# One-core graph network on edge ends: projections written out without loops, aggregations with a narrow end-row product and byte masks

## The reference, cut to what matters

```python
x = x + L0(relu(layernorm(x)))   # 3 rounds: h = h + sigmoid(GAT(h)), one head
x = x + L1(relu(layernorm(x)))   # relational conv, 4 bases
x = x + L2(relu(layernorm(x)))   # GAT, 8 heads, linear
x = x + L3(relu(layernorm(x)))   # edge messages and mean
# GAT(x): h = x @ W; s = h @ a_src; d = h @ a_dst
#   e = leaky(s[src] + d[dst]), softmax over the edges of each dst and a self loop
#   out[n] = sum(alpha * h[src]) + alpha_self * h[n] + b
```

## Time and profile before

| | us |
|---|---|
| median of three runs | 4129.71 (4114.74 to 4135.91) |
| the profiled execution | 4123.5 |
| its span, first to last instruction | 4121.8 |
| TensorE, VectorE, ScalarE, GpSimd busy | 2421.4, 2277.9, 1509.5, 2159.3 |

### The profile page before, as it was taken

The page is one execution under the profiler, slowest core; times in us unless marked ns, Lnnn a source line. Parts: engine busy times, 40 slices in busy tenths (PEclk is TensorE's granted clock), DMA queues, the critical chain, the costliest instruction groups (busy, mean ns, idle before and its releaser), DMA issues. The chain is left out here.

```text
span 4121.8 us, 57885 instructions
## 1 busy us (share of the span) xinstructions
PE 2421.4 (59%) x13649; PEld 1953.8 (47%) x13649; DVE 2277.9 (55%) x7669; ACT 1509.5 (37%) x3239; POOL 2159.3 (52%) x1921
## 2 busy tenths in 40 slices
PE   1136899999996647466465637775636444433433
PEld 1123676667676546466454634454626332322222
DVE  3145999899896655223423448885674333333223
ACT  0006999999994641121122013222420022222100
POOL 3628675557645850350064236555820278877755
PEclk9998999999998875686588559887865576666655
DMA  2140132333212537441654363323312533333243
GB/s 61 31 167 24 47 103 88 90 96 106 88 51 67 143 100 228 140 123 47 177 152 109 112 187 95 95 86 87 111 29 81 151 74 72 73 70 72 53 137 114
DMA packets 570788, 405.84 MB, mean 98 GB/s; under 512 B 51549, under 2 KB 497702, under 8 KB 570146
## 3 DMA queue, kind: packets, MB, share of 16 engines
q1 hardware_dynamic: 513650, 356.21, 28.7%
q0 software_dynamic: 56000, 46.29, 6.0%
q10 hardware_dynamic: 880, 0.41, 0.0%
HBM read 270.38 MB, written 158.24 MB: 104 GB/s over the span
## 5 line engine op out<-in xcount | busy, mean ns | idle before, releaser
L1147 POOL DMA_INDIRECT p_ends_state<-t_d,p_ends_ix x300 | 316.0, 1053 | 568.0 <-issue 279.7
L806 POOL TENSOR_TENSOR a_rs<-a_ve,w_neg_half 128x16 f32<-128x16 f32 x113 | 330.4, 2924 | 243.1 <-DVE a_ve L742 211.8
L1367 PE MATMUL p_pm<-w_aug,p_ht 128*128 128x130 f32 (+1 forms) x1600 | 327.9, 326 | 165.1 <-ACT p_ht L1321 107.4
L832 ACT ACTIVATE a_nr<-a_xb,a_nm,a_rs 128x128 f32<-128x128 f32 x882 | 370.4, 488 | 26.1 <-POOL a_nm L808 26.1
L1972 POOL DMA_INDIRECT e_a<-t_d,e_ix x200 | 209.4, 1047 | 298.1 <-DMA e_a<-t_s 235.9
L1367 PEld LDWEIGHTS p_pm<-w_aug,p_ht 128*128 128x128 f32 x1600 | 272.0, 231 | 187.0 <-issue 135.1
L894 PE MATMUL a_ps<-w_ident,a_nr 128*128 128x128 f32 x1568 | 247.7, 282 | 126.7 <-ACT a_ht L840 47.0
L902 PE MATMUL a_ps<-a_ht,w_aug 128*128 128x512 f32 x588 | 316.8, 624 | 2.4 <-DVE a_ht L709 2.4
L894 PEld LDWEIGHTS a_ps<-w_ident,a_nr 128*128 128x128 f32 x1568 | 181.9, 144 | 275.8 <-issue 243.1
L1697 PE MATMUL c_ps<-layer_src,c_sel 128*128 (+1 forms) x800 | 192.0, 419 | 192.3 <-DMA c_sel<-t_sel 107.8
L709 DVE TENSOR_TENSOR a_ht<-a_ps,a_ht 128x512 f32<-128x512 f32 x294 | 201.9, 688 | 135.2 <-ACT a_ps L847 117.8
(11 more groups left out here) (362 smaller groups left out, 6724.9 us busy)
## 6 DMA issues: line engine op xcount, KB each, us to landing
t_s<-p_ends_state SPq DMA_DIRECT2D x100, 256.0 KB
c_sel<-t_sel SPq DMA_DIRECT2D x100, 256.0 KB
c_a<-t_d SPq DMA_DIRECT2D x100, 256.0 KB
t_d<-c_a SPq DMA_DIRECT2D x100, 256.0 KB
a_xa<-in_x SPq DMA_DIRECT2D x98, 256.0 KB
out<-a_xb SPq DMA_DIRECT2D x98, 256.0 KB, 2.0
p_ends_state<-t_s SPq DMA_DIRECT2D x75, 256.0 KB
p_ends_state<-t_d SPq DMA_DIRECT2D x75, 256.0 KB
```

The lines of the kernel that those rows point to most:

```text
L806: nc.gpsimd.tensor_tensor(RS[:, z, :], VE[:, z, :], w["neg_half"][:, None, 0:J].to_broadcast([P, LNS, J]), ALU.pow).then_inc(s_rstd.sem, 1)
L832: last = nc.scalar.activation(NR[k][:, T.at(NORM[k], 2), cols(j)], normed_rows(T, k)[:, cols(j)], ACT.Identity, bias=NM[:, T.at(1, SHORT), ...
L1147: eng.indirect_dma_start(out=self.A[:, g, SRC, j, :], out_offset=None, in_=self.t[self.dst_table], in_offset=bass.IndirectOffsetOnAxis(ap= ...
L1367: last = nc.tensor.matmul(PM[side][:, j, 0:CW], HT[:, g, side, j * C:(j + 1) * C], rhs, start=side == SRC, stop=True)
```

## The change

`project` is written out for all 25 blocks without a loop. Its state ring has 7 slots, its other rings 3. The gathers read `map_ix` directly, without VectorE's copy. A new class `Moments` takes the reciprocal root on VectorE by Newton steps (12 steps put between the statistics of the next block) in place of GpSimd's `pow`; ScalarE applies both sides' norms, in "first" with the relu in the same instruction; VectorE adds the bias for both sides, and the identity products are gone. The order of VectorE's turn n is statistics of n with the Newton steps of n-1, residual of n-4, products of n-3; SyncE stores block b and then loads block b+6.

In `aggregate` the end-row product swaps its operands: `end_of` (now 8 columns a tile) is stationary and the kept rows stream, accumulated over the 4 tiles of a block. ScalarE copies the small result, and ten DMAs on its queue bring it and the tiles' own end rows to `ENDT`. The own rows are scaled ahead of the loop, for one head 13 of 25 blocks by ScalarE. The mask is stored as bytes (64 KB a block) and widened by ScalarE; the store of block n-3 follows the loads of n. The gathers of `maps` (100, on GpSimd) move from p0 into c0, and `rows_found` runs after c0.

```diff
+def newton(self, eng, b, step):
+    v, g = self.nc.vector, b % self.ring
+    ve, half, square, y = self.var_eps[:, g, :], self.half[:, g, :], self.square[:, g, :], self.rstd[:, g, :]
+    if step == 0:
+        eng.wait_ge(self.s_moments, b + 1)
+        v.tensor_scalar(ve, self.moments[:, g, :, 1], LN_EPS, None, ALU.add).then_inc(self.s_newton, 1)
+        return
+    eng.wait_ge(self.s_newton, b * (self.STEPS - 1) + step)
+    if step == 1:
+        v.tensor_scalar(half, ve, -0.5, None, ALU.mult)
+        v.tensor_scalar(y.bitcast(I32), ve.bitcast(I32), -0.5, 1597463007.0, ALU.mult, ALU.add).then_inc(self.s_newton, 1)
+    elif step == self.STEPS - 1:
+        v.scalar_tensor_tensor(self.shift[:, g, :], self.moments[:, g, :, 0], -1.0, y, ALU.mult, ALU.mult).then_inc(self.s_shift, 1)
+    elif step % 3 == 2:
+        v.tensor_tensor(square, y, y, ALU.mult).then_inc(self.s_newton, 1)
+    elif step % 3 == 0:
+        v.tensor_tensor(square, square, half, ALU.mult).then_inc(self.s_newton, 1)
+    else:
+        v.scalar_tensor_tensor(y, square, 1.5, y, ALU.add, ALU.mult).then_inc(self.s_newton, 1)
...
+def turn(self, eng, rows, b, last):
+    v = self.nc.vector
+    step = 0
+    for n in range(self.n):
+        if b <= last:
+            ins_ = v.bn_stats(self.stats[:, b % self.ring, n, :], rows(n))
+            if n == self.n - 1:
+                ins_.then_inc(self.s_stats, 1)
+        if b and step < self.STEPS:
+            self.newton(eng, b - 1, step)
+            step += 1
+    if b <= last:
+        eng.wait_ge(self.s_stats, b + 1)
+    for n in range(self.n):
+        if b <= last:
+            ins_ = v.bn_aggr(self.moments[:, b % self.ring, n, :], self.stats[:, b % self.ring, n, :])
+            if n == self.n - 1:
+                ins_.then_inc(self.s_moments, 1)
+        if n % 2 and b and step < self.STEPS:
+            self.newton(eng, b - 1, step)
+            step += 1
+    assert not b or step == self.STEPS
...
+RING, SHORT = 7, 3
...
+def load(b):
+    g = b % RING
+    if b >= RING:
+        eng.wait_ge(s_out[g], (uses(b) - 1) * OUTS)
+        eng.wait_ge(s_mm[DST], b - RING + 1)
+    for side in (SRC, DST):
+        eng.dma_start(A[:, g, side, :, :], block_rows(t[tables[side]], b)).then_inc(s_load[g], 16)
+def load_x(b):
+    if b >= SHORT:
+        eng.wait_ge(s_plus, b - SHORT + 1)
+    eng.dma_start(XS[:, b % SHORT, :, :], block_rows(t["xs"], b)).then_inc(s_xs[b % SHORT], 16)
+def store(b):
+    g = b % RING
+    if first:
+        eng.wait_ge(s_normed[DST], b + 1)
         eng.dma_start(block_rows(t["d0"], b), A[:, g, DST, :, :]).then_inc(s_out[g], 16)
+    eng.wait_ge(s_next, b + 1)
     eng.dma_start(block_rows(t[f"s{r + 1}"], b), A[:, g, SRC, :, :]).then_inc(s_out[g], 16)
...
+    for b in range(RING):
+        load(b)
+        if plus_x and b < SHORT:
+            load_x(b)
+    for b in range(BLOCKS):
+        store(b)
+        if b and b - 1 + RING < BLOCKS:
+            load(b - 1 + RING)
+        if plus_x and b + SHORT < BLOCKS:
+            load_x(b + SHORT)
+    for g in range(RING):
+        eng.wait_ge(s_out[g], OUTS * len(range(g, BLOCKS, RING)))
+if overlay:
+    @block.gpsimd
+    def _(eng):
+        for b in range(BLOCKS):
+            g = b % RING
+            eng.wait_ge(s_load[g], uses(b) * 32)
+            for j in range(J):
+                eng.indirect_dma_start(out=A[:, g, SRC, j, :], out_offset=None, in_=t[f"d{r}"],
+                                       in_offset=bass.IndirectOffsetOnAxis(ap=k["map_ix"][:, b * J + j:b * J + j + 1], axis=0),
+                                       bounds_check=EP - 1, oob_is_err=False).then_inc(s_over[g], 16)
...
+wide = BR[:, None, :].to_broadcast([P, J, CW])
+def hold(b):
+    for side in (SRC, DST):
+        eng.wait_ge(s_mm[side], b + 1)
+        v.tensor_tensor(held(("src", "dst")[side], b)[:, :, 0:CW], PM[side][:, :, 0:CW], wide, ALU.add).then_inc(s_keep[side], 1)
+def residual(b):
+    g, grow = b % RING, UP[:, b % SHORT, :, :] if sigmoid else held("src", b)[:, :, 0:C]
+    if sigmoid:
+        eng.wait_ge(s_sig, b + 1)
+    else:
+        eng.wait_ge(s_keep[SRC], b + 1)
+    if plus_x:
+        eng.wait_ge(s_xs[b % SHORT], (b // SHORT + 1) * 16)
+        v.tensor_tensor(grow, grow, XS[:, b % SHORT, :, :], ALU.add).then_inc(s_plus, 1)
+        eng.wait_ge(s_plus, b + 1)
+    there(eng, b, SRC)
+    v.tensor_tensor(A[:, g, SRC, :, :], A[:, g, SRC, :, :], grow, ALU.add).then_inc(s_next, 1)
+holds, residuals = (3, 4) if norm else (0, 1)
+for n in range(BLOCKS + residuals):
+    if norm and n <= BLOCKS:
+        if n < BLOCKS:
+            there(eng, n)
+        mo.turn(eng, lambda m: A[:, n % RING, m // J, m % J, :], n, BLOCKS - 1)
+    if 0 <= n - residuals:
+        residual(n - residuals)
+    if 0 <= n - holds < BLOCKS:
+        hold(n - holds)
...
+def apply(b):
+    g, m = b % RING, b % SHORT
+    eng.wait_ge(mo.s_shift, b + 1)
+    if normed and b >= SHORT:
+        eng.wait_ge(s_mm[DST], b - SHORT + 1)
     for side in (SRC, DST):
+        for j in range(J):
+            n = side * J + j
+            rows = A[:, g, side, j, :]
+            last = nc.scalar.activation(NR[:, m, side, j, :] if normed else rows, rows, ACT.Identity if normed else ACT.Relu,
+                                        bias=mo.shift[:, m, n:n + 1], scale=mo.rstd[:, m, n:n + 1])
+        last.then_inc(s_normed[side], 1)
+def copy(b):
     for side in (SRC, DST):
+        eng.wait_ge(s_tp, b * 2 + side + 1)
+        if b >= SHORT:
+            eng.wait_ge(s_mm[side], b - SHORT + 1)
+        nc.scalar.activation(HT[:, b % SHORT, side, :], PT[b % 2][side][:, :, :].rearrange("p j c -> p (j c)"),
+                             ACT.Relu if normed else ACT.Copy).then_inc(s_ht, 1)
+def squash(b):
+    eng.wait_ge(s_keep[SRC], b + 1)
+    if b >= SHORT:
+        eng.wait_ge(s_next, b - SHORT + 1)
+    nc.scalar.activation(UP[:, b % SHORT, :, :], held("src", b)[:, :, 0:C], ACT.Sigmoid).then_inc(s_sig, 1)
+copies, squashes = (1, 2) if norm else (0, 1)
+for n in range(BLOCKS + squashes):
+    if norm and n < BLOCKS:
+        apply(n)
+    if 0 <= n - copies < BLOCKS:
+        copy(n - copies)
+    if sigmoid and 0 <= n - squashes:
...
+def turn(b):
     for side in (SRC, DST):
+        if norm:
+            eng.wait_ge(s_normed[side], b + 1)
         else:
+            there(eng, b, side)
+        if b >= 2:
+            eng.wait_ge(s_ht, (b - 2) * 2 + side + 1)
         for j in range(J):
+            rows = NR[:, b % SHORT, side, j, :] if normed else A[:, b % RING, side, j, :]
+            last = nc.tensor.transpose(PT[b % 2][side][:, j, :], rows, w["ident"][:, :])
         last.then_inc(s_tp, 1)
+def product(b):
     for side in (SRC, DST):
+        eng.wait_ge(s_ht, b * 2 + side + 1)
+        if b:
+            eng.wait_ge(s_keep[side], b)
         for j in range(J):
+            last = nc.tensor.matmul(PM[side][:, j, 0:CW], HT[:, b % SHORT, side, cols(j)], rhs, start=True, stop=True)
+        last.then_inc(s_mm[side], 1)
+products = 1 if norm else 0
+for n in range(BLOCKS + products):
+    if n < BLOCKS:
+        turn(n)
+    if 0 <= n - products:
+        product(n - products)
...
+ON_ACT = 13 if H == 1 else 0
+in_bank = lambda n: range(n * J, min(n * J + J, BLOCKS))
     def load(b, g):
-        wait(eng, s_pe, b - GE + 1)
-        carry_waits(eng, w)
-        eng.dma_start(SEL[:, g, :, :].rearrange("p j q -> p (j q)"), sel_rows(b)).then_inc(s_sel_in[g], 16)
+        if first:
+            wait(eng, s_sel, b - GE + 1)
+            carry_waits(eng, w)
+            eng.dma_start(KB[:, g, :, :].rearrange("p j q -> p (j q)"),
+                          t["dst_row"][0:1, bass.ds(number(b) * (J * P), J * P)].to_broadcast([P, J * P])).then_inc(s_kb[g], 16)
+        else:
+            wait(eng, s_wide, b - GE + 1)
+            carry_waits(eng, w)
+            eng.dma_start(SEL8[:, g, :, :].rearrange("p j q -> p (j q)"), sel_rows(b)).then_inc(s_sel_in[g], 16)
         wait(eng, s_out[g], (b // GE) * 16)
         carry_waits(eng, w)
         eng.dma_start(A[:, g, :, :], block_rows(t[f"d{r}"], b)).then_inc(s_load[g], 16)
         if plus_x:
             eng.dma_start(XD[:, g, :, :], block_rows(t["xd"], b)).then_inc(s_xd[g], 16)
...
+def store_sel(b, g):
+    wait(eng, s_sel, b + 1)
+    carry_waits(eng, w)
+    eng.dma_start(sel_rows(b), SEL8[:, g, :, :].rearrange("p j q -> p (j q)")).then_inc(s_sel_out[g], 16)
 def store(b, g):
     wait(eng, s_next, b + 1)
     carry_waits(eng, w)
     eng.dma_start(block_rows(t[f"d{r + 1}"], b), A[:, g, :, :]).then_inc(s_out[g], 16)
-stream(eng, (load, 0), (store, 4))
+stream(eng, (load, 0), *([(store_sel, 2)] if first else []), (store, 3))
 for g in range(GE):
     eng.wait_ge(s_out[g], 16 * ROUNDS_E)
+    if first:
...
+if first:
+    s_found = sem("found")
+    @block.gpsimd
+    def _(eng):
+        for n in range(T):
```

(102 more changed lines are left out.)

216 lines of the change are left out of this document (44 added, 172 removed).

## The result

The changed kernel took 4066.7 us (median of four, 4058.6 to 4070.6) against 4122.2 of before: ratio 0.9859, interval 0.9824 to 0.9894. It is faster by 1.4%; 5.5% were forecast. The profiled execution took 4066.8.

The account below looks back on a forecast made before the run. No engine bounds the whole; each stage has its own bound, such as GpSimd's gathers or a store's landing. 28 + 45 + 42 + 0 + 12 + (9 + 9 + 10) + (22 + 31 + 22) - 2 = 228; 4123.5 - 228 = 3896 us, range 3840 to 4003.

Parts of the forecast that it names:

- Second and third projection: 5.6 us a block, above GpSimd's gather floor of 5.2, from 7.03 before: -45 and -42 us.
- a ring of 7 holds 2 x 5.2 us more, about the longest wait: Second and third projection: 7 state slots in place of 5 absorb waits up to 12.3 us, giving 5.6 a block.
- Rival 1: Waits of the second and third projection stay: +45 + 42, 3983 us in all; chance 0.15.
- The fourth rival: Fetching the written-out code makes the kernel slower: 51 x 7.8 = 397 us, 4293 in all; chance 0.05.
- First aggregation: 100 map gathers move here, 130 us at 1.30 plus 7 for start and landing: 137 against 149, -12.
- Last projection: GpSimd loses 2 us a block but the state ring holds turns at 7.7: 204 against 207.4, taken as 0.
- The ring: Last projection: residual, store, reload, gathers and landing must fit in two turns; 7.5 to 8.5 us a turn, 7.7 taken.
- 2P: Last projection: two turns from a block's residual to the reloaded slot's statistics, 15.1 to 17.1 us, load landing 4.2.
- First projection: Roots move to VectorE; its turn is 6.5 us (5.8 to 7.5), Newton operations 0.13 each: 175 of 203, -28.
- End rows: Last three aggregations: product 23 us, ten DMAs 6.2, landing 3.2, end products 1.9 and tail: -9, -9, -10.
- rival 2: TensorE's clock stays at 0.50 in the new end product: +15.5 in each of three, +7 in the first, 3950; chance 0.14.
- Main loops: Second to fourth aggregation: later stores spread landings, 2.8 us a turn from 3.9 (third 3.3 from 4.9): -22, -31, -22.

Follow-up runs that it names:

- The fourth experiment: The changed kernel, but in the last projection VectorE adds the residual of block n-3 in place of n-4; 3743.8 us on time, kernel before beside it 3940.9.
- the last version: The changed kernel with residual a turn earlier, 40 map gathers in the first projection, and a GpSimd memset between gathers; ratio to before 0.949 on time, 0.968 late.

## Why the prediction was wrong, step by step

- **Second and third projection (-45, -42; got -13, -5).** The failing step is "a ring of 7 holds 2 x 5.2 us more, about the longest wait". The waits of the earlier trace rows were late posts, which the ring did not absorb. The first residual add comes 40 us into the second projection, for 21 forecast, while the ring's first 28 gathers (20 before) run back to back; after it the adds come every 6.0 us in the mean, with gaps of 12 to 16 (in the third 6.3, up to 20), for 5.6 forecast. That the longer first run made the waits grow (their gaps were 11 at most before) is argued, not shown. Rival 1 had their persistence at 87 us; 69 were lost. On time the first add comes 22 us in and the adds 5.2 apart, the bare pace of the gathers; the two stages take 149 to 155 there, for 157 forecast. The fourth rival, code fetch, is not supported: the same written-out code takes these times on time. The Trainium skill, "Runtime: NRT & Kernel Launch", Instruction fetch mechanics, says that instructions are fetched ahead in order, hidden behind their issue, and that a taken branch can break this; the times on time agree with it.
- **First aggregation (-12; got +74).** "130 us at 1.30, beside 149 in which GpSimd was idle" was right for GpSimd and blind for the rest: the move put gathers back to back beside a loop that exchanges about a dozen posts a turn. That is 82 us of the 223 (141 with roots in their place on a late chip). The stage's own chain, put at 129, was short as well: it takes these 141. The earlier trace rows gave no price, as the stage of before that had the map gathers was held by GpSimd anyway.
- **Last projection (0; got +36).** The ring was rightly named and its term too small. SyncE, then GpSimd:

```profile
2888.08 0.38 SPq L1282 DMA_DIRECT2D t_s<-p_a  x1
2888.56 0.45 SPq L1269 DMA_DIRECT2D p_a<-t_s  x1
2889.05 0.56 SPq L1269 DMA_DIRECT2D p_a<-t_d  x1
...
2894.29 1.00 POOL L1304 DMA_INDIRECT p_a<-t_d,k_map_ix  x1 [4.66 <-DMA p_a<-t_d]
2898.21 1.00 POOL L1304 DMA_INDIRECT p_a<-t_d,k_map_ix  x1 [0.30 <-issue]
```

  The second load lands after 5.2 us, not 4.2, and adds come every 8.7, not 7.7: 2P is 17.4, above my 17.1. That is 18 us over 18 turns and is there on time too (226). Some 17 more are the start, where 28 gathers stretch the Newton steps and the first add comes 57 us in (37 on time).
- **First projection (-28; got -47).** The Newton steps were mis-sized: 0.06 to 0.07 each between statistics, not 0.13. A turn of VectorE is 4.9, and turns of 4.9 and 6.1 to 6.8 alternate, 5.6 in the mean, under the lower end of 5.8.
- **End rows (-9 each).** Right. The new end product ran at a granted clock of 0.71 in its first 5 us and of 1.00, the 2.4 GHz level, after that, so rival 2 did not come; the rows of TensorE and of L1692:

```profile
1923.24 23.28 PE L1754 MATMUL c_pq<-layer_src,k_end_of 128*8 128x128 f32 x200 [2.04 <-DVE layer_src L1685]
1959.58 0.42 DVE L1692 TENSOR_TENSOR c_new<-c_pn,c_endt 100x256 f32<-100x256 f32 x1 [14.72 <-PE c_pn L1760]
```

  23.3 us for 200 (forecast 23), and L1692 is 37 us into the stage (38 to 39 forecast; the four terms named add to 36.9). By the Trainium skill, "TensorE: Matmul & The Clock Gate", Part 1, activity of TensorE releases the throttled clock. The measurement differs for the 4-column product, 99% busy at 0.50, and agrees for this one.
- **Main loops (-22, -31, -22).** Right in the second and third, 5 us short in the last: these stages total 116, 123 and 118 for 115, 124 and 113. Stores in the second lie 2.8 apart in the mean (1991.40, 1994.20, 1997.74, 1999.91, 2002.61 on SyncE).

The misses: 86 + 32 + 37 + 36 over, 19 under, 5 over in the last aggregation: 177, for 171 between 3896 and 4066.8; the rest lies in the short stages between.

On time the change was not timed as a whole. The fourth experiment plus the last projection's 45 us gives 3743.8 + 45 = 3789, of 3940.9: 0.961. That is worked out, not measured. By it the change gains 152 us there, not the 228 forecast: the forecast set out from stages of before that late posts had already lengthened, and how long these are on time was not profiled.

## What to carry to other kernels

A wait whose named releaser makes no sense, after an instruction long done, is itself a finding: price it by where it occurs before moving more of what runs there. On some chips, gathers back to back beside stages that exchange many posts cost far more than GpSimd's own time; spread them over stages with slack, as the 40 in the first projection. Time before and after on more than one chip. Count a ring's round trip with the landing of the last load, and move the step that frees a slot ahead in its turn.

## What the runs showed of the hardware that was not expected

Six chips fell in two kinds, 3935 to 3942 us and 4092 to 4132 us for the same kernel (the last version: 3738.8 and 3977.8). On the slower kind, during gathers 1.30 us apart, a VectorE step that waits for its own engine's post took 1.4 to 2.8 us instead of 0.27, and TensorE's posts came up to 40 us after the product; the gathers themselves kept 1.30. With `pow` on GpSimd in place of the gathers no post was late. Why a chip is of one kind, and by what way gathers delay posts, is not known.
